# W's transfer ahead of x's, both halves of W's square ahead of x's transposes, and a shorter fourth product of zeros

## The chip, the cores and the metric

The kernel runs on one core of a Trainium2 chip. The metric is the device time of one execution in microseconds (us); a kernel's figure is the median of its runs. TensorE (PE, with its weight loads PEld), VectorE (DVE), ScalarE (ACT) and GpSimd (POOL) compute; SyncE (SP) and ACT issue the transfers here.

## The reference, cut to what matters

x is 128 rows of 256, the context 12544 rows of 256 and W a matrix of 256 by 256. The change lies in the preparation of the first stage, a cross-attention in which queries and keys are projected by the same W and b:

```python
def _L0_xattn_ref(ix, iother, W, b):      # ix = layernorm(x), iother = ctx_1024
    ex = jnp.einsum('bld,ed->ble', ix, W) + b
    eother = jnp.einsum('bld,ed->ble', iother, W) + b
    scores = jnp.einsum('bld,bmd->blm', ex, eother)
    attn = jax.nn.softmax(scores, axis=-1)
    return jnp.einsum('blm,bmd->bld', attn, iother)

x = x + _L0_xattn_ref(_layernorm(x), ctx_1024, W, b)
x = x + _L0_attn_ref(_layernorm(x), proj_w, proj_b, filter_time)   # two gated convolutions
x = x + _L0_ffn_ref(_layernorm(x), norm_g, ..., Wg, bg, Wu, bu, Wd, bd)   # 16 soft experts
```

## The kernel before

The kernel has three stages on 128 partitions. The cross-attention walks the 12544 context rows in 25 groups of up to four tiles of 128 rows, with a running maximum. Instead of projecting every key it projects the queries by WᵀW: `square_W(d)` (L387 to L392) forms half d of WᵀW, with one more column, 256, that gives Wᵀb; for that `W_sb` has 257 columns, of which the last is b, copied there by DVE (L1041, semaphore `bcol_set`). Each half is four records on TensorE in the profile: two products of float32, each recorded twice. ACT copies the first half out of bank 6 with its sign turned (L795), DVE the second half out of bank 7 (L1055); each raises `WW_rdy`. x is normed on DVE (`norm`, L1034 to L1044) with a power on POOL in its middle (`power`, L991), transposed on TensorE (`transpose_xh`, L260 to L266), and copied by DVE into `xhT` (L1053). The query product (L477 to L481) waits for both copies of WW and for `xhT`.

Every engine has its own program, written out by hand; instructions of one engine run in the order written and engines meet at semaphores. The order on TensorE (from L382): four products of zeros into bank 7, each 128 by 256, which only wait for a memset of `zero` (L383 to L385) and whose result nobody reads; then a wait for W's transfer (`ld_W`) and for `bcol_set`, half 0 of the square, a wait for the identity's transfer (`ld_ident`), the two transposes of the normed x (which wait for `xh_rdy`), half 1 of the square, then the transposes of context group 0 (`transpose_ctx`, L474), the query product, the transposes of group 1, and so on. ACT splits group 0's transposes into a high part (`cT_hi`, L807), DVE into a low part (`cT_lo`, L1083); the transposes of group 1 write the same banks 0 and 1 and wait for `cT_lo`.

On SP's queue the order is x (128 KB), W (256 KB), context group 0 (512 KB), then a wait for `ld_W`, groups 1 to 3, the slot embeddings, the filter and the tables (L282 to L297). ACT's queue carries the columns (b among them), the identity and the scale (L783 to L785). POOL's order is memsets, the power of x's norm, then the high and low rows of each group (L1000, L1005). The order on DVE around the change: memsets, x's norm with the copy of b between its parts, the copy of `xhT`, the copy of WW's second half, then `cT_lo` of group 0.

```python
            pe.wait_ge(ld_W, 16)
            pe.wait_ge(bcol_set, 1)
            square_W(0)
            pe.wait_ge(ld_ident, 16)
            transpose_xh(pe, 0)
            square_W(1)
            ...
            transpose_ctx(None, 0, 0)
            pe.wait_ge(WW_rdy, DK)
            pe.wait_ge(xhT_rdy, 1)
```

Of the kernel before, what the change touches and what calls it, by code (L numbers as in the profile page):

```python
# [13 lines left out]
def perceiver_kernel(nc, x, ctx_in, xattn_W, proj_w, proj_b, filter_time, norm_g, norm_b,  # L14
# [3 lines left out]
    ALU = mybir.AluOpType  # L18
# [3 lines left out]
    P = 128  # L22
    D = x.shape[2]
# [28 lines left out]
    with st:  # L52
        def sem(name):
            return st.enter_context(nc.semaphore(name))

        def sb(name, shape, dt=fp32, where=st):
            return where.enter_context(nc.sbuf_tensor(name, shape, dt))

        bank = [st.enter_context(nc.psum_tensor(f"bank{i}", [P, 512], fp32)) for i in range(8)]
# [15 lines left out]
        zero = sb("zero", [P, 1])  # L75
        col = sb("col", [P, 5, DK])
# [44 lines left out]
        W_sb = sb("W_sb", [P, DK, D + 1], fp32, pre)  # L121
        WW = sb("WW", [P, DK, D + 1], fp32, pre)
# [42 lines left out]
        ld_x, ld_W, ld_tab, ld_scale = sem("ld_x"), sem("ld_W"), sem("ld_tab"), sem("ld_scale")  # L165
        ld_se, ld_col, ld_row, ld_filt = sem("ld_se"), sem("ld_col"), sem("ld_row"), sem("ld_filt")
# [12 lines left out]
        WW_ps, WW_rdy = sem("WW_ps"), sem("WW_rdy")  # L179
        bcol_set, bb_rdy, minus_set = sem("bcol_set"), sem("bb_rdy"), sem("minus_set")  # L180
# [79 lines left out]
        def transpose_xh(pe, n):  # L260

            if n == 0:
                pe.wait_ge(xh_rdy, 1)
                for k in range(DK):
                    last = nc.tensor.transpose(bank[XH_BANK[0]][:, k * P:(k + 1) * P], xh[:, k * P:(k + 1) * P], ident)
                last.then_inc(xhT_ps, 1)  # L266
            else:

                for k in range(DK):
                    pe.wait_ge(xh_rdy, k + 2)  # L270
                    nc.tensor.transpose(bank[XH_BANK[1][k]][:, 0:P], xh[:, k * P:(k + 1) * P], ident
                                        ).then_inc(xhT_ps, 1)
# [6 lines left out]

        @block.sync  # L280
        def _(sp):
            sp.dma_start(x_sb[:, :], x[0, :, :]).then_inc(ld_x, 16)  # L282
            sp.dma_start(W_sb[:, :, 0:D], xattn_W.rearrange("(k p) d -> p k d", p=P)).then_inc(ld_W, 16)

            def load_rows(g):
                sp.dma_start(raw[:, g % RING, 0:tiles_of(g), :], ctx_v[:, g * GT:g * GT + tiles_of(g), :]
# [88 lines left out]
        def _(pe):  # L375
# [4 lines left out]


            pe.wait_ge(const_set, 1)  # L382
            for _ in range(4):  # L383
                nc.tensor.matmul(bank[7][:, 0:D], zero[:, 0:1].broadcast_to([P, P]), zero[:, 0:1].broadcast_to([P, D]),  # L384
                                 start=True, stop=True)  # L385

            def square_W(d):  # L387

                for e in range(DK):
                    last = nc.tensor.matmul(bank[6 + d][:, 0:D + 1], W_sb[:, e, d * P:(d + 1) * P], W_sb[:, e, :],  # L390
                                            start=(e == 0), stop=(e == DK - 1))
                last.then_inc(WW_ps, 1)  # L392

            pe.wait_ge(ld_W, 16)
            pe.wait_ge(bcol_set, 1)
            square_W(0)
            pe.wait_ge(ld_ident, 16)
            transpose_xh(pe, 0)
            square_W(1)
            def spectrum(o):  # L400

                pe.wait_ge(ld_filt, 16)
                pe.wait_ge(ld_tab, 16)
                nc.tensor.matmul(bank[4 + o][:, 0:D], dft_s, filt[:, o, :], start=True, stop=True)
                nc.tensor.matmul(bank[4 + o][:, D:2 * D], dft_c, filt[:, o, :], start=True, stop=True
                                 ).then_inc(spec_ps, 1)
# [614 lines left out]
        def _(dve):  # L1021
# [8 lines left out]
            def mean_and_variance(src):  # L1030
                link(nc.vector.bn_stats(stat6[:, :], src))
                link(nc.vector.bn_aggr(mv[:, :], stat6[:, :]))

            def norm(n, src, dst, done):  # L1034

                mean_and_variance(src)
                nc.vector.tensor_scalar(mv[:, 1:2], mv[:, 1:2], EPS, None, ALU.add).then_inc(var_rdy, 1)
                if n == 0:

                    dve.wait_ge(ld_col, 16)  # L1040
                    nc.vector.tensor_copy(W_sb[:, :, D], col[:, 0, :]).then_inc(bcol_set, 1)  # L1041
                dve.wait_ge(rstd_rdy, n + 1)
                nc.vector.tensor_scalar(dst, src, mv[:, 0:1], rstd[:, 0:1], ALU.subtract, ALU.mult
                                        ).then_inc(done, 1)  # L1044
# [2 lines left out]
            nc.vector.memset(minus[:, :], -1.0).then_inc(minus_set, 1)  # L1047
            nc.vector.memset(negm[:, RING - 1:RING], BIG)
            nc.vector.memset(c_hi[:, :, :, D:D + 2].bitcast(fp32), 1.0).then_inc(one_set, 1)
            dve.wait_ge(ld_x, 16)  # L1050
            norm(0, x_sb[:, :], xh[:, :], xh_rdy)
            dve.wait_ge(xhT_ps, 1)
            nc.vector.tensor_copy(xhT[:, :, :].rearrange("p k t -> p (k t)"), bank[XH_BANK[0]][:, 0:D]).then_inc(xhT_rdy, 1)  # L1053
            dve.wait_ge(WW_ps, 2)
            nc.vector.tensor_scalar(WW[:, 1, :], bank[7][:, 0:D + 1], -1.0, None, ALU.mult).then_inc(WW_rdy, 1)  # L1055

# [309 lines left out]
```

## Time and profile before

| | |
|---|---|
| median of 3 runs | 193.16 us (192.81 to 194.14) |
| the profiled execution's own time | 193.59 us |
| its span, first to last instruction | 191.5 us |
| PE / PEld busy | 187.1 us (98%) / 146.8 us (77%) |
| DVE / ACT / POOL busy | 125.7 / 108.8 / 82.3 us |
| DMA | 47.01 MB, mean 245 GB/s |

Some 2.1 us of an execution lie outside the span. A busy PE counts overlapping records of pipelined matmuls, whose ends are modelled; the starts of successive records are the better measure of pace, and this document steps from start to start.

### The profile page before, as it was taken

The page shows a single profiled execution, that of the slowest core. Times are in us where ns is not written, and L with a number is a line of the kernel's source. Part 1 is how long each engine was busy: PE and PEld are TensorE (multiplying, and loading weights), DVE is VectorE, ACT ScalarE, POOL GpSimd, SP SyncE. Part 2 cuts the span into 40 slices and gives each one's busy share as a digit, 9 for nine tenths or more (in the row PEclk, how much of TensorE's full clock was granted, in tenths as well). Part 3 has the DMA queues.
Part 4 walks back from the last instruction along what each step waited for, and adds up shares of the span by engine and source line. Part 5 has one row for each costly group of instructions (what it writes and reads, how often), then busy time and mean ns, then how long its engine had stood idle before and what let it go on. Part 6 is the DMA issues. An engine that isn't in the chain of part 4 may idle for free.

```text
span 191.5 us, 3972 instructions
## 1 busy us (share of the span) xinstructions
PE 187.1 (98%) x1270; PEld 146.8 (77%) x1270; DVE 125.7 (66%) x272; ACT 108.8 (57%) x226; POOL 82.3 (43%) x61
## 2 busy tenths in 40 slices
PE   8999999999999999999999999999999999999995
PEld 5888999999999999999999989974544545454463
DVE  3376997797778779777778788753673513524542
ACT  3558778777777776776775542967358521112210
POOL 2678879778778768877868013100000000000000
DMA  6999958857874774985594299999999999992200
GB/s 183 317 364 334 336 162 265 264 179 219 237 241 158 272 262 147 324 225 161 154 235 106 74 381 379 354 371 369 381 364 383 285 348 296 282 216 79 83 0 27
DMA packets 25051, 47.01 MB, mean 245 GB/s; under 512 B 1616, under 2 KB 12112, under 8 KB 25040
## 3 DMA queue, kind: packets, MB, share of 16 engines
q1 hardware_dynamic: 23808, 43.52, 70.2%
q10 hardware_dynamic: 1232, 3.35, 7.1%
q8 instruction: 6, 0.10, 0.2%
q14 instruction: 5, 0.04, 0.1%
HBM read 46.73 MB, written 0.13 MB: 245 GB/s over the span
## 4 chain that ended last, share of the span: by engine, by line
PE 95%; ACT 2%; DVE 1%; issue 0%; POOL 0%; ACTq 0%; POOLq 0%
PE bank L670 15%; PE bank L415 11%; PE bank L684 6%; PE bank L456 6%; PE bank L460 6%; PE bank L458 6%; PE bank L428 6%; PE bank L432 6%; PE bank L430 6%; PE bank L441 6%; PE bank L732 2%; PE bank L722 2%; PE bank L384 2%; PE bank L557 2%; PE bank L576 2%; ACT seT L888 1%
## 5 line engine op out<-in xcount | busy, mean ns | idle before, releaser
L1005 POOL TENSOR_TENSOR c_lo<-raw,c_hi 128x1024 fp32r<-128x1024 f32 (+1 forms) x25 | 53.9, 2156 | 20.9 <-ACT c_hi L801 20.9
L1083 DVE TENSOR_TENSOR cT_lo<-bank,cT_hi 128x512 fp32r<-128x512 f32 (+1 forms) x50 | 31.7, 674 | 9.7 <-ACT cT_hi L828 8.6
L828 ACT ACTIVATE cT_hi<-bank 128x512 fp32r<-128x512 f32 (+1 forms) x48 | 25.6, 584 | 9.8 <-PE bank L415 9.7
L456 PE MATMUL bank<-c_hi,pT_hi 128*128 128x258 f32 x98 | 30.0, 306 | 0.0
L460 PE MATMUL bank<-c_hi,pT_lo 128*128 128x258 f32 x98 | 27.7, 283 | 0.0
L458 PE MATMUL bank<-c_lo,pT_hi 128*128 128x256 f32 x98 | 27.6, 281 | 0.0
L1000 POOL TENSOR_TENSOR c_hi<-raw,zero 128x512 fp32r<-128x512 f32 (+1 forms) x25 | 25.6, 1025 | 1.5 <-DMA raw<-in_ctx_dram 1.5
L415 PE MATMUL bank<-tab,raw 128*128 128x128 f32 x196 | 25.6, 273 | 0.2 <-DVE cT_lo L1083 0.2
L835 ACT ACTIVATE pT_hi<-bank 128x512 fp32r<-128x512 f32 (+1 forms) x25 | 14.7, 590 | 14.5 <-PE bank L441 14.5
L415 PEld LDWEIGHTS bank<-tab,raw 128*128 128x128 f32 x196 | 22.1, 141 | 0.8 <-issue 0.3
L428 PE MATMUL bank<-cT_hi,q_hi 128*128 128x512 f32 (+1 forms) x50 | 21.5, 430 | 0.0
L1101 DVE TENSOR_TENSOR pT_lo<-bank,pT_hi 128x512 fp32r<-128x512 f32 (+1 forms) x25 | 17.0, 679 | 5.2 <-ACT pT_hi L835 5.0
L1095 DVE TENSOR_SCALAR_CACHE_REDUCE nsc<-bank,s,negm 128x512 f32<-128x512 f32 (+1 forms) x25 | 19.8, 793 | 0.8 <-PE bank L432 0.7
L843 ACT ACTIVATE prob<-nsc,negm 128x512 f32<-128x512 f32 (+1 forms) x25 | 17.7, 710 | 3.3 <-DVE nsc L1095 2.9
L432 PE MATMUL bank<-cT_hi,q_lo 128*128 128x512 f32 (+1 forms) x50 | 19.5, 390 | 0.0
L430 PE MATMUL bank<-cT_lo,q_hi 128*128 128x512 f32 (+1 forms) x50 | 19.3, 386 | 0.0
L458 PEld LDWEIGHTS bank<-c_lo,pT_hi 128*128 128x128 f32 x98 | 18.7, 191 | 0.0
L460 PEld LDWEIGHTS bank<-c_hi,pT_lo 128*128 128x128 f32 x98 | 18.5, 189 | 0.0
L456 PEld LDWEIGHTS bank<-c_hi,pT_hi 128*128 128x128 f32 x98 | 18.5, 189 | 0.0
L801 ACT ACTIVATE c_hi<-raw 128x512 fp32r<-128x512 f32 (+1 forms) x25 | 15.6, 625 | 0.0
L670 PE MATMUL bank<-early_gu,slots_or_se 128*64 128x512 f32 x64 | 15.2, 600 | 0.0
L1111 DVE SCALAR_TENSOR_TENSOR O<-O,alpha,bank 128x258 f32<-128x258 f32 x25 | 12.1, 482 | 4.3 <-PE bank L460 2.9
(178 smaller groups left out, 292.7 us busy)
## 6 DMA issues: line engine op xcount, KB each, us to landing
raw<-in_ctx_dram SPq DMA_DIRECT2D x24, 512.0 KB, 3.9
bias<-biases_dram ACTq DMA_DIRECT2D x10, 320.0 KB, 7.5
late_gu<-in_L_ffn_Wg_dram SPq DMA_DIRECT2D x3, 1024.0 KB, 10.5
late_gu<-in_L_ffn_Wu_dram SPq DMA_DIRECT2D x3, 1024.0 KB, 11.2
late_d<-in_L_ffn_Wd_dram SPq DMA_DIRECT2D x3, 1024.0 KB, 13.7
early_gu<-in_L_ffn_Wg_dram SPq DMA_DIRECT2D x4, 512.0 KB, 4.7
early_gu<-in_L_ffn_Wu_dram SPq DMA_DIRECT2D x4, 512.0 KB, 4.6
early_d<-in_L_ffn_Wd_dram SPq DMA_DIRECT2D x4, 512.0 KB, 5.0
```

Source lines behind the costliest of these rows:

```text
L415: last = nc.tensor.transpose(bank[h][:, t * P:(t + 1) * P], raw[:, slot, t, h * P:(h + 1) * P], ident)
L428: nc.tensor.matmul(bank[2 + r][:, 0:n], q_hi[:, h, :], cT_hi[:, r, h, 0:n], start=(h == 0), stop=False)
L430: nc.tensor.matmul(bank[2 + r][:, 0:n], q_hi[:, h, :], cT_lo[:, r, h, 0:n], start=False, stop=False)
L432: last = nc.tensor.matmul(bank[2 + r][:, 0:n], q_lo[:, h, :], cT_hi[:, r, h, 0:n], start=False, stop=(h == DK - 1))
L456: nc.tensor.matmul(bank[6 + r][:, 0:D + 2], ph, c_hi[:, slot, t, :], start=(t == 0), stop=False)
L458: nc.tensor.matmul(bank[6 + r][:, 0:D], ph, c_lo[:, slot, t, :], start=False, stop=False)
L460: last = nc.tensor.matmul(bank[6 + r][:, 0:D + 2], pl, c_hi[:, slot, t, :], start=False, stop=(t == nt - 1))
L670: last = nc.tensor.matmul(bank[b][a * SL:(a + 1) * SL, :], slotsT[:, k, p * P + a * SL:p * P + (a + 1) * SL], w_gu(s, which, a, a + 1)[:, ...
L828: nc.scalar.activation(cT_hi[:, g % 2, h, 0:n], bank[h][:, 0:n], ACT.Copy).then_inc(cThi_rdy, 1)
L1000: nc.gpsimd.tensor_tensor(c_hi[:, slot, 0:nt // 2, 0:D], raw[:, slot, 0:nt // 2, :], zero[:, 0:1].unsqueeze(2).broadcast_to([P, nt // 2, D ...
L1005: nc.gpsimd.tensor_tensor(c_lo[:, slot, 0:nt, :], raw[:, slot, 0:nt, :], c_hi[:, slot, 0:nt, 0:D].bitcast(fp32), ALU.subtract).then_inc(cl ...
L1083: nc.vector.tensor_tensor(cT_lo[:, g % 2, h, 0:n], bank[h][:, 0:n], cT_hi[:, g % 2, h, 0:n].bitcast(fp32), ALU.subtract).then_inc(cTlo_rdy, 1)
```

## The change

W's transfer is issued before x's on SP. On TensorE the fourth product of zeros streams 64 columns instead of 256, and half 1 of the square comes before the transposes of x. On DVE the copy of b into `W_sb` comes before the wait for x, and the copy of WW's second half before the copy of `xhT`. Transfers, products and copies are otherwise the same ones.

```diff
         def _(sp):
+            sp.dma_start(W_sb[:, :, 0:D], xattn_W.rearrange("(k p) d -> p k d", p=P)).then_inc(ld_W, 16)
             sp.dma_start(x_sb[:, :], x[0, :, :]).then_inc(ld_x, 16)
-            sp.dma_start(W_sb[:, :, 0:D], xattn_W.rearrange("(k p) d -> p k d", p=P)).then_inc(ld_W, 16)
...
             pe.wait_ge(const_set, 1)
-            for _ in range(4):
-                nc.tensor.matmul(bank[7][:, 0:D], zero[:, 0:1].broadcast_to([P, P]), zero[:, 0:1].broadcast_to([P, D]),
+            for w in (D, D, D, P // 2):
+                nc.tensor.matmul(bank[7][:, 0:w], zero[:, 0:1].broadcast_to([P, P]), zero[:, 0:1].broadcast_to([P, w]),
                                  start=True, stop=True)
...
             square_W(0)
+            square_W(1)
             pe.wait_ge(ld_ident, 16)
             transpose_xh(pe, 0)
-            square_W(1)
...
                 nc.vector.tensor_scalar(mv[:, 1:2], mv[:, 1:2], EPS, None, ALU.add).then_inc(var_rdy, 1)
-                if n == 0:
-
-                    dve.wait_ge(ld_col, 16)
-                    nc.vector.tensor_copy(W_sb[:, :, D], col[:, 0, :]).then_inc(bcol_set, 1)
...
+            dve.wait_ge(ld_col, 16)
+            nc.vector.tensor_copy(W_sb[:, :, D], col[:, 0, :]).then_inc(bcol_set, 1)
             dve.wait_ge(ld_x, 16)
             norm(0, x_sb[:, :], xh[:, :], xh_rdy)
+            dve.wait_ge(WW_ps, 2)
+            nc.vector.tensor_scalar(WW[:, 1, :], bank[7][:, 0:D + 1], -1.0, None, ALU.mult).then_inc(WW_rdy, 1)
             dve.wait_ge(xhT_ps, 1)
             nc.vector.tensor_copy(xhT[:, :, :].rearrange("p k t -> p (k t)"), bank[XH_BANK[0]][:, 0:D]).then_inc(xhT_rdy, 1)
-            dve.wait_ge(WW_ps, 2)
-            nc.vector.tensor_scalar(WW[:, 1, :], bank[7][:, 0:D + 1], -1.0, None, ALU.mult).then_inc(WW_rdy, 1)
```

## Rows read from the trace of the kernel before

**Rows 1.** The page: the chain that ended last, by engine.

```profile
PE 95%; ACT 2%; DVE 1%; issue 0%; POOL 0%; ACTq 0%; POOLq 0%
```

**Rows 2.** Waits of PE's matmuls over the whole span: total us, times, longest.

```profile
PE bank L384 <- POOL neg_half L985: 0.9, 1, 0.9
PE bank L518 <- ACT xhT L877: 0.3, 1, 0.3
...
PE bank L415 <- DVE cT_lo L1083: 0.2, 1, 0.2
```

**Rows 3.** Timeline of PE, 0 to 20 us: start, us, line, tiles, count [idle before].

```profile
0.90 3.78 PE L384 MATMUL bank<-zero 128*128 128x256 f32 x8 [0.90 <-POOL neg_half L985]
...
6.46 1.03 PE L390 MATMUL bank<-W_sb 128*128 128x257 f32 x4
7.34 1.04 PE L415 MATMUL bank<-tab,raw 128*128 128x128 f32 x8
8.21 1.06 PE L479 MATMUL bank<-xhT,WW 128*128 128x128 f32 x8
9.44 1.16 PE L415 MATMUL bank<-tab,raw 128*128 128x128 f32 x8 [0.17 <-DVE cT_lo L1083]
10.44 0.50 PE L487 MATMUL bank<-WW,xhT 128*128 128x1 f32 x4
...
11.25 0.48 PE L428 MATMUL bank<-cT_hi,q_hi 128*128 128x512 f32 x1
```

**Rows 4.** Timelines of PE over short windows: the starts of single records.

```profile
3.62 1.06 PE L384 MATMUL bank<-zero 128*128 128x256 f32 x2
...
4.04 0.64 PE L384 MATMUL bank<-zero 128*128 128x256 f32 x1
4.48 0.50 PEld L390 LDWEIGHTS bank<-W_sb 128*128 128x128 f32 x2 [0.53 <-DMA W_sb<-in_L_xattn_W_dram]
...
5.07 1.07 PE L390 MATMUL bank<-W_sb 128*128 128x257 f32 x2
...
5.93 0.48 PE L390 MATMUL bank<-W_sb 128*128 128x257 f32 x1
6.25 0.27 PE L265 MATMUL bank<-tab,xh 128*128 128x128 f32 x1
```

**Rows 5.** Timeline of DVE, 0 to 20 us.

```profile
2.86 0.43 DVE L1031 BATCH_NORM_STATS2 stat<-x_sb 128x6 f32<-128x256 f32 x1 [1.52 <-DMA x_sb<-in_x_dram]
...
4.43 0.41 DVE L1043 TENSOR_SCALAR xh<-x_sb,mv,rstd 128x256 f32<-128x256 f32 x1 [0.67 <-POOL rstd L991]
...
7.54 0.42 DVE L1055 TENSOR_SCALAR WW<-bank 128x257 f32<-128x257 f32 x1 [0.45 <-PE bank L390]
8.60 1.29 DVE L1083 TENSOR_TENSOR cT_lo<-bank,cT_hi 128x512 fp32r<-128x512 f32 x2 [0.64 <-ACT cT_hi L807]
```

**Rows 6.** Timelines of POOL and ACT in the same stretch.

```profile
5.91 1.04 POOL L1000 TENSOR_TENSOR c_hi<-raw,zero 128x512 fp32r<-128x512 f32 x1 [1.51 <-DMA raw<-in_ctx_dram]
...
7.97 1.08 ACT L807 ACTIVATE cT_hi<-bank 128x512 fp32r<-128x512 f32 x2 [0.62 <-PE bank L415]
```

**Rows 7.** Timeline of SP's queue: when transfers are issued.

```profile
0.75 0.39 SPq L282 DMA_DIRECT2D x_sb<-in_x_dram  x1
1.20 0.42 SPq L283 DMA_DIRECT2D W_sb<-in_L_xattn_W_dram  x1
```

**Rows 8.** DMA issues, 0 to 14 us: KB each, us from issue to landing.

```profile
W_sb<-in_L_xattn_W_dram SPq DMA_DIRECT2D x1, 256.0 KB, 3.2
...
x_sb<-in_x_dram SPq DMA_DIRECT2D x1, 128.0 KB, 2.1
tab<-tables_dram ACTq DMA_DIRECT2D x1, 64.0 KB, 3.3
col<-columns_dram ACTq DMA_DIRECT2D x1, 5.0 KB, 2.3
```

**Rows 9.** Busy time by stretch; the last three columns: granted clock, DMA share, GB/s.

```profile
2.00:3.00 1.00, 1.00 (x4) 0.82 (x3) 0.14 (x1) 0.81 (x1) 0.00 (x0) 1.00 0.92 144
```

## The prediction

> **What bounds the kernel now.** I read the chain of work that ended last first: TensorE carries 95% of the span [rows 1]. Then the waits of its matmuls: the listed ones are five, none over 0.3 us after the start, and none of them is for a transfer [rows 2]. So what is gained or lost ahead of the steady loop over the context groups should reach the end, and only TensorE's own time counts, or a stall of it. That sends the reader to its timeline over the first 20 us [rows 3]: it works without a gap from 0.90 us to the transposes of group 1 at 9.44, where it waits 0.17 us for the low part of group 0.
>
> The second thing to see is its pace. The granted clock is shown as 1.00 throughout [rows 9], but equal records tell otherwise. Products of 256 or 257 columns start 0.42 to 0.43 us apart before 6 us (3.62 to 4.04; 5.07 to 5.93 for two [rows 4]) and the four records of the square's second half take 6.46 to about 7.34, 0.22 us each [rows 3]. That is TensorE at 1.2 GHz and then at 2.4 GHz. The last slow record starts at 5.93 and the transpose behind it at 6.25: 0.32 us, a mixture of both paces. With a share s at 0.43 and the rest at 0.217, s/0.43 + (0.32 - s)/0.217 = 1 gives s = 0.21, so the clock rose at about 6.14 us, after 5.24 us of work. A microsecond saved in front of that moment is filled with other slow work until it comes: only half of it is left behind it, if the moment itself stands still.
>
> The third thing is W. The weight load of the square's first record waits 0.53 us for the transfer and starts at 4.48; the next record starts at 5.07, 0.59 us after it and not 0.43 [rows 4]. A load that waits can't be done ahead, which costs 0.16 us. W is issued at 1.20 and lands 3.2 us later, at 4.40; x is issued at 0.75 and lands 2.1 us later, at 2.85 [rows 7, 8].
>
> **The fourth product of zeros.** Its two records start at 3.62 and 4.04 [rows 4], together 0.85 us. With 64 columns the stream would be a quarter, 0.107 us each. But every record also loads 128 columns of weights, which doesn't shrink. The nearest rows for that floor are the products with one column: eight records (L487 and L489, four each) start between 10.44 and 11.25, 0.10 us each at 2.4 GHz [rows 3], so 0.20 at 1.2 GHz. I take the floor: 2 x 0.20 = 0.41, a saving of 0.44 us at the slow pace; the other bound is 0.85 - 0.21 = 0.64. The zeros then end at 3.62 + 0.41 = 4.03 us. The Trainium skill ("TensorE: Matmul & The Clock Gate", LDWEIGHTS) prices a load by its columns alone, 128/1.2 = 107 ns, which would be no floor here and give the 0.64; the rows of this kernel show 0.10 us already at the full clock for a float32 record with almost no stream, so I stay with them.
>
> **W first.** Issued at 0.75 in place of 1.20, W lands at 0.75 + 3.2 = 3.95 us at the latest, if being first in the queue saves nothing. If it does: x, half its size, landed after 2.1 us, and the second 128 KB take another 0.9 us at the 144 GB/s that the stretch from 2 to 3 us moved [rows 9]: 0.75 + 2.1 + 0.9 = 3.75 us. The lower bound is x's own landing, 2.85. I take 3.75. The column b, which used to be copied in the middle of x's norm, needs its own transfer: ACT issues it first, it takes 2.3 us [rows 8], and DVE is free until x comes, so the copy of two elements per partition is done near 3.3 us. Both are then there before the load of the square's first record can begin (3.83, when the last zero record starts), and the 0.16 us goes as well. The square's second record starts at 4.03 + 0.43 = 4.46 in place of 5.07: 0.61 us earlier, all at the slow pace. With W at 3.95 it starts at 3.95 + 0.59 = 4.54, 0.53 us earlier. With no gain of W at all it starts at 5.07 as before: the zeros are only filler, and the whole saving hangs on W.
>
> **Both halves before the transposes.** This moves work and removes none. By 6.14 us, (6.14 - 4.03)/0.433 = 4.87 of the square's eight records are done; the other 3.13 take 0.68 us at 0.217, to 6.82; the two transposes take 0.21 us (6.25 to 6.46 [rows 3, 4]), to 7.03. The transposes of group 0 then start at 7.03 and not at 7.34: a gain of 0.30 us, half of 0.61.
>
> **What is later, and what hides it.** x is now behind W in the queue. It lands at 3.3 us at the earliest (1.20 + 2.1) and at 4.40 at the latest, since both transfers together were through by then. From landing to the normed x it takes 2.86 to 4.84, 1.98 us, with the power on POOL in it [rows 5]; so the normed x is there between 5.3 and 6.4 us. The cover is the square, until 6.82: 0.4 us at least. Without it TensorE would stand until 6.4, and POOL's power, queued ahead of group 0's high rows at 5.91 [rows 6], would hold those by under 0.1 us, which ACT's later half hides (POOL's low part needs ACT's rows as well). The identity is unmoved and lands at 4.5, 3.3 us after its issue on ACT [rows 8].
>
> DVE has two copies of 0.42 us in a row: WW's second half from 7.03 (0.2 us behind the last record, as now: 7.34 to 7.54 [rows 3, 5]) to 7.45, then `xhT` to 7.87. The query product waits for both. TensorE reaches it at 7.03 + 0.87 = 7.90 (7.34 to 8.21 [rows 3]), and a waiting weight load costs up to 0.2 us: 8.1 us, ending by 9.0. Behind it stand the transposes of group 1, which must wait anyway for `cT_lo` of group 0: that chain runs from the transposes of group 0 over ACT at 7.97 and DVE at 8.60 to 9.44 [rows 3, 5, 6], and all of it moves up by the 0.30, to 9.14. So the small stall lies inside a wait that exists, and I cost it at nothing. ACT copies the first half of WW earlier than before. Groups 1 to 3 are issued behind the wait for `ld_W`, some 0.6 us earlier; TensorE waits for none of them now, and group 0 is issued third as before. From 9.44 on TensorE has no wait of its own until the next stage [rows 2], so the 0.30 stays to the end.
>
> **The sum.** 193.59 - 0.30 = 193.29 us for the profiled execution, which lies 0.43 above the median of the runs; against that median 193.16 - 0.30 = 192.86, say 192.9 us. Bounds of the mechanism: 0.26 (half of 0.53) to 0.80 (0.64 + 0.16, if the clock doesn't rise until all of it is banked).
>
> **Rivals.** *Nothing gained*: W's landing is set by what else the engines carry (the identity, the columns and group 0 share them), or TensorE waits for x or for DVE instead. For it: W took 3.2 us though its bytes are few. Against it: x alone landed 1.55 us before W. The start of the square stays at 4.48, and the time at 193.2.
>
> *The clock rises later.* The zeros are there to keep TensorE at work; with a shorter fourth one the activity in front of 6.14 is thinner (two records that mostly load weights), and where W comes late it even stands still from 4.03 on. If that starts the count anew, the clock rises 5.24 us after 4.03, at 9.3 us and not at 6.14; the 3.1 us run at half pace, a loss of 1.57, less the 0.30: +1.3, or 194.4 us. Being over 1% slower would need 4.5 us more at 1.2 GHz. Against it: the load of W's first record at 4.48 left a thin place too, and the clock rose all the same. The Trainium skill ("TensorE: Matmul & The Clock Gate", Why this matters for your kernels) advises keeping TensorE at work without a pause until its clock is released, which speaks against shortening filler; no row here shows a rise missed for one short product.
>
> *The clock rises earlier.* The gap at W's load and the transposes are out of the first 6 us, which is then denser in products. If the clock rose as early as 4.03, (6.14 - 4.03)/2 = 1.05 us would come on top of 0.30: 191.8 us, still not 1% faster. But x would then be needed at 5.8 us and could be late, taking back up to 0.6. No row speaks for a rise that early.
>
> **How the numbers follow.** Forecast, 0.26 to 0.80 faster: 0.62. Nothing gained: 0.18. Later rise, 194.4: 0.12. Earlier rise, 191.8: 0.06. Something unnamed: 0.02. The runs of before spread from 0.35 below to 0.98 above their median. The range takes in the forecast's far bound with the spread below, 193.16 - 0.80 - 0.35 = 192.0, and the no-gain case with the spread above, 193.16 + 0.98 = 194.1. It leaves out the last three cases, 0.20. About 1% (1.9 us) is what a measurement of this kernel can tell from no change. No named case crosses it on either side; the tails of the clock's rivals give 0.03 faster and 0.04 slower, and 0.93 stays within 1%.
>
> **What the profile would show.** Right: SP's first transfer is W, landed by 3.95; the last zero record 0.2 us after the one before it; the square's first record near 4.0 with no weight load waiting for W; eight records of the square in a row, then the transposes of x near 6.8 with no wait for x; group 0's transposes near 7.0, group 1's near 9.1, and every later start 0.3 us earlier. Wrong: a wait of TensorE for W until 4.4, or for x; group 1's transposes gated by the query product; or records of the square, of group 0 or of the queries at the slow pace beyond 6.2 us.

## The result, and the profile after

The changed kernel takes 194.31 us (median of 18 runs, 193.65 to 194.66), the kernel before 193.22 us (median of 18 runs, 192.72 to 194.14). The ratio is 1.0045, with a 95% interval of 1.0033 to 1.0058: slower by some 0.9 us (the means of the runs differ by 0.92, the medians by 1.09), where 0.3 us faster was forecast. The profiled execution took 194.36 us with a span of 192.3 us, 0.77 and 0.8 us above those of before.

The timeline of PE of the changed kernel, 0 to 20 us:

```profile
0.90 3.25 PE L384 MATMUL bank<-zero 128*128 128x256 f32 x8 [0.90 <-POOL neg_half L985]
3.94 2.70 PE L390 MATMUL bank<-W_sb 128*128 128x257 f32 x8
6.48 0.41 PE L265 MATMUL bank<-tab,xh 128*128 128x128 f32 x2
8.00 1.09 PE L415 MATMUL bank<-tab,raw 128*128 128x128 f32 x8 [1.12 <-DMA raw<-in_ctx_dram]
8.93 1.06 PE L479 MATMUL bank<-xhT,WW 128*128 128x128 f32 x8
10.17 1.16 PE L415 MATMUL bank<-tab,raw 128*128 128x128 f32 x8 [0.17 <-DVE cT_lo L1082]
```

Down to 6.48 us this is what was forecast, and better: no pause before W, the square in one piece from 3.94, the transposes of x at 6.48 with no wait. Then TensorE, which would have been at group 0 by 6.7, stands 1.12 us for the transfer of group 0. Its transposes start at 8.00 in place of 7.34, those of group 1 at 10.17 in place of 9.44 [rows 3], and 0.73 us is, within 0.1, what the span has grown.

The rest of the kernel follows that start closely. In 13 of the 20 profiles of this study the span ends 184.2 to 184.3 us after group 0's transposes begin, whatever the order of the transfers (191.5 - 7.34 before, 192.3 - 8.00 here); in the other seven group 1 was late too, or TensorE's clock was still low. So the start of these transposes is the figure to compare. By it the kernel before, at its median of 193.22 us, has them near 6.9 us (an estimate: 193.22 less the 2.1 us outside the span, less 184.2); its profiled execution, with 7.34, was one of its slower ones. The changed kernel has them at 8.0 by its median too.

The chain that ended last, for the first 11 us (start, us, what), shows the same from the other end:

```profile
0.75 0.45 SPq L282
...
1.26 0.47 SPq L283
...
1.78 6.18 DMA raw<-in_ctx_dram
...
8.00 0.67 PE bank L415 x4
```

The chain of before was on TensorE from 0.90 us. Now it runs through SP's first two issues and the third transfer, group 0: 6.18 us from issue to landing. In the kernel before, POOL, which was waiting for it, could start on group 0 at 5.91 [rows 6]. SP's queue and the landings of W and x in the changed kernel (the second fence is the list of issues: KB each, us to landing):

```profile
0.75 0.45 SPq L282 DMA_DIRECT2D W_sb<-in_L_xattn_W_dram  x1
1.26 0.47 SPq L283 DMA_DIRECT2D x_sb<-in_x_dram  x1
3.84 1.28 SPq L286 DMA_DIRECT2D raw<-in_ctx_dram  x3
5.16 0.65 SPq L294 DMA_DIRECT2D slots_or_se<-n_L_ffn_slot_embeds_dram  x1
```

```profile
W_sb<-in_L_xattn_W_dram SPq DMA_DIRECT2D x1, 256.0 KB, 3.1
x_sb<-in_x_dram SPq DMA_DIRECT2D x1, 128.0 KB, 3.1
```

W lands at 3.85 and frees SP's wait behind group 0: groups 1 to 3 are issued from 3.84 us on. In the kernel before W landed at 4.40 [rows 7, 8], and the same stretch of SP's timeline reads:

```profile
4.45 1.28 SPq L286 DMA_DIRECT2D raw<-in_ctx_dram  x3
```

So two things have changed around group 0: W's longer transfer goes ahead of x's, and three transfers of 512 KB are issued 0.6 us sooner behind it. The busy table by stretch (last columns: granted clock, DMA share, GB/s) shows that the engines moved less while group 0 was due; first the changed kernel, then the one before:

```profile
4.00:5.00 1.00, 1.00 (x4) 0.81 (x4) 0.61 (x2) 0.06 (x1) 0.00 (x0) 1.00 0.51 176
5.00:6.00 1.00, 1.00 (x5) 0.86 (x4) 0.24 (x2) 0.19 (x1) 0.56 (x1) 1.00 1.25 291
```

```profile
4.00:5.00 1.00, 1.00 (x3) 0.50 (x2) 0.41 (x1) 0.06 (x1) 0.40 (x1) 1.00 1.00 389
5.00:6.00 1.00, 1.00 (x4) 0.74 (x3) 0.00 (x0) 0.00 (x0) 0.09 (x1) 1.00 0.86 140
```

Between 4 and 5 us, when most of group 0 must have come in before (W landed at 4.40 and group 0 by 5.9), the changed kernel moves 176 GB/s in place of 389.

### The profile page after: what moved, and what is told of

It reads as the page before. It is cut to its first block, busy times and chain, and to the rows that moved or that the text cites. A ratio compares the mean times of both kernels' runs of the same rounds, so it can differ in the third digit from the quotient of the medians.

```text
span 192.3 us, 3972 instructions
## 1 busy us (share of the span) xinstructions
PE 186.7 (97%) x1270; PEld 146.6 (76%) x1270; DVE 125.7 (65%) x272; ACT 108.9 (57%) x226; POOL 82.3 (43%) x61
## 4 chain that ended last, share of the span: by engine, by line
PE 92%; DMA 3%; ACT 2%; DVE 1%; SPq 0%; issue 0%; ACTq 0%
PE bank L670 15%; PE bank L415 11%; PE bank L684 6%; PE bank L456 6%; PE bank L460 6%; PE bank L458 6%; PE bank L428 6%; PE bank L432 6%; PE bank L430 6%; PE bank L441 6%; DMA raw<-in_ctx_dram 3%; PE bank L732 2%; PE bank L722 2%; PE bank L557 2%; PE bank L576 2%; ACT seT L888 1%
```

## The experiments

The theory to test: the loss is group 0's landing, and that is late through the order of transfers, not through TensorE's new order or the shorter product. Within it two causes compete: (A) the issue of groups 1 to 3 at 3.8 in place of 4.45 us, and (B) W's transfer ahead of x's by itself. The landings of group 0 below are the starts of the first instructions that waited for it; where none waited (d1, d4, f1) they are the issue plus the time that the list of issues gives. "Changed" and "before" are the two kernels of this document; ratios are to the kernel before, from the same chip.

**Is it the order of transfers?** Two kernels take the change apart.

```diff
 # c1_swap: the kernel before, with
+            sp.dma_start(W_sb...)      # ahead of x
             sp.dma_start(x_sb...)
 # and on DVE, ahead of the wait for x
+            dve.wait_ge(ld_col, 16)
+            nc.vector.tensor_copy(W_sb[:, :, D], col[:, 0, :]).then_inc(bcol_set, 1)
```

> The kernel before with only W's transfer ahead of x's, and the copy of b into W_sb ahead of the wait for x (without it the square would wait for x). TensorE's order and the four full products of zeros are those of before. Theory (W first, or what is issued behind it, makes group 0 late): group 0 lands near 8.0 us as in the changed kernel and not at 5.9, TensorE waits for it up to 1.1 us, the time is 0.6 to 1.1 us above before. Rival (TensorE's new order or the shorter product is at fault): group 0 lands by 6.3, and the time is within 0.2 us of before.

194.04 us, ratio 1.0036 (1.0017 to 1.0054). Group 0 lands at 7.70. But TensorE's long wait is another one here: the transposes of x still stand between the halves of the square, and x is late.

```profile
4.47 1.38 PE L390 MATMUL bank<-W_sb 128*128 128x257 f32 x4
6.45 0.41 PE L265 MATMUL bank<-tab,xh 128*128 128x128 f32 x2 [0.60 <-DVE xh L1039]
7.68 1.09 PE L415 MATMUL bank<-tab,raw 128*128 128x128 f32 x8
```

TensorE waits 0.60 us for the normed x; group 0, landed at 7.70, costs it only some 0.1 on top. But the two waits cover each other: without the first, TensorE would have been at group 0 by 7.0 and waited there instead, so it is still group 0's landing that sets the 7.68. The swap costs time without the rest of the change. The expected size came out; the expected wait of up to 1.1 us shows as two.

```diff
 # c2_no_swap: the changed kernel, with
             sp.dma_start(x_sb...)
+            sp.dma_start(W_sb...)      # behind x again
```

> The changed kernel with x's transfer ahead of W's again; the shorter product and both halves of the square ahead of the transposes stay. Theory (the order of transfers is the cause): group 0 lands at about 5.9, TensorE does not wait for it, and the time is that of before within 0.3 us. Rival (the order on TensorE): the time stays about 0.9 us above before.

193.56 us, ratio 1.001 (0.9982 to 1.0038). Group 0 lands at 6.13, no wait for it; TensorE stands 0.32 us for W.

```profile
4.47 2.76 PE L390 MATMUL bank<-W_sb 128*128 128x257 f32 x8 [0.32 <-DMA W_sb<-in_L_xattn_W_dram]
...
7.29 1.04 PE L415 MATMUL bank<-tab,raw 128*128 128x128 f32 x8
```

The changed kernel differs from this one by the swap alone, and it is what loses. The loss is gone with the swap, and so is the gain: TensorE's new order and the shorter product alone bring nothing that this can measure.

**Which of the two causes?**

```diff
 # c3_hold_next: the changed kernel
             load_rows(0)
             sp.wait_ge(ld_W, 16)
+            sp.wait_ge(ld_raw[0], 16)
             load_rows(1)
```

> The changed kernel, but SP issues groups 1 to 3 only when group 0 has landed. Theory A (groups 1 to 3, issued 0.6 us earlier than before behind the wait for W, share the DMA engines with group 0): group 0 lands at 6.0 to 6.5, its transposes start by 7.1, and the time is 0.8 to 1.1 us below the changed kernel unless group 1 is then late. Theory B (W's longer transfer ahead holds group 0 itself): group 0 still lands at 7.5 to 8 and the time is that of the changed kernel or worse.

196.62 us (six runs, 194.56 to 198.06), ratio 1.0115 (1.0068 to 1.0162). Group 0 lands at 7.13: between the two answers. Holding the others back gives 0.9 of the 2.1 us and leaves 1.2 over the kernel before (d3 below, with the same hold, brings what W ahead of x costs down to 0.5). Group 1, issued at 7.19, is then late, and behind that pause TensorE's clock falls:

```profile
11.14 1.09 PE L416 MATMUL bank<-tab,raw 128*128 128x128 f32 x8 [2.00 <-DMA raw<-in_ctx_dram]
...
13.67 0.63 PE L431 MATMUL bank<-cT_lo,q_hi 128*128 128x512 f32 x1
14.10 0.63 PE L433 MATMUL bank<-cT_hi,q_lo 128*128 128x512 f32 x1
```

Products of 512 columns start 0.43 us apart behind the 2.00 us wait; the same two start 0.24 us apart in the changed kernel (12.29 and 12.53). That is 1.2 GHz again (granted clock 0.50 from 13 to 15 us). The length of the pause alone does not decide it: in d1 and d4 below, waits of 2.21 and 2.48 us have no such fall behind them.

```diff
 # c4_no_hold: the kernel before
             load_rows(0)
-            sp.wait_ge(ld_W, 16)
             load_rows(1)
```

> The kernel before without SP's wait for W ahead of group 1, so that groups 1 to 3 are issued from about 2.2 us on; transfer order and all else as before. Theory A (early issue of groups 1 to 3 delays group 0): group 0 lands at 7.5 us or later, TensorE waits for it, the time is 0.8 us or more above before. Theory B (W ahead of x is what delays group 0): group 0 lands near 5.9 and the time is within 0.2 us of before.

193.97 us, ratio 1.0039 (1.0017 to 1.006). With x first and all as before, but groups 1 to 3 issued from 2.17 us on, group 0 is late too:

```profile
7.53 1.09 PE L414 MATMUL bank<-tab,raw 128*128 128x128 f32 x8 [0.68 <-DMA raw<-in_ctx_dram]
```

So early issue alone can delay group 0 from 5.91 to 7.5 us (A), though these issues are 1.7 us earlier than the changed kernel's, and the time was expected 0.2 us higher than it came.

```diff
 # d2_hold_x: the changed kernel
             sp.wait_ge(ld_W, 16)
+            sp.wait_ge(ld_x, 16)
             load_rows(1)
```

> The changed kernel with SP waiting for x as well as for W ahead of group 1: groups 1 to 3 are issued at about 4.35 us, where the kernel before issues them at 4.45 us. If the early issue alone costs the time, group 0 lands near 6 and the time is within 0.3 us of before or below it. If W ahead of x costs by itself, group 0 lands between 7.1 (what holding groups 1 to 3 to the end gave) and 7.7, and the time is 0.4 to 0.7 us above before.

193.8 us, ratio 1.0034 (1.0005 to 1.0062). Groups 1 to 3 are issued at 4.33, and group 0 lands at 6.80, between the two answers and 1.2 us earlier than in the changed kernel, for issues 0.5 us later; its transposes start at 7.02 with no wait for it or for x.

```profile
5.85 0.41 DVE L1040 TENSOR_SCALAR xh<-x_sb,mv,rstd 128x256 f32<-128x256 f32 x1 [0.74 <-POOL rstd L992]
7.02 1.04 PE L416 MATMUL bank<-tab,raw 128*128 128x128 f32 x8
6.84 1.04 POOL L1001 TENSOR_TENSOR c_hi<-raw,zero 128x512 fp32r<-128x512 f32 x1 [1.03 <-DMA raw<-in_ctx_dram]
10.96 1.09 PE L416 MATMUL bank<-tab,raw 128*128 128x128 f32 x8 [1.92 <-DMA raw<-in_ctx_dram]
```

The 7.02 is what the prediction had forecast (7.03), with the clock rising near 6.0 as it had assumed. But this execution (196.64 us, the highest of the twelve) then waits 1.92 us for group 1. Nine of the twelve lie between 193.24 and 194.20. The lateness can move from group 0 to group 1; what holds the nine back no profile shows.

```diff
 # d3_before_hold: the kernel before
             sp.wait_ge(ld_W, 16)
+            sp.wait_ge(ld_raw[0], 16)
             load_rows(1)
```

> The kernel before with groups 1 to 3 held until group 0 has landed: the same hold as in the changed kernel, now with x ahead of W. If W ahead of x costs by itself, group 0 lands here at 5.5 to 6.0 against 7.1 there. If not, it lands at about 7 here too. Group 1 is then late in either case, and the whole time 1.5 to 3 us above before.

196.02 us (one run). Group 0 lands at 6.60, between the answers again and 0.7 us later than in the kernel before, though nothing is issued behind it before 6.65. The hold itself need not be the cause: between 4.00 and 4.25 us, before it acts, the engines moved 98 GB/s here and 360 in the kernel before. Against 7.13 with W first it is still 0.5 us earlier.

```diff
 # e1_hold_23: the changed kernel; e2_before_hold_23: before; e3_no_swap_hold_23: changed, x first
             load_rows(1)
+            sp.wait_ge(ld_raw[0], 16)
             load_rows(2)
```

> The changed kernel; SP issues group 1 behind the wait for W as there, but groups 2 and 3 and all behind them only when group 0 has landed. If it is the mass of groups 2, 3 and the slot embeddings that holds group 0, group 0 lands near 7.0 us, group 1 near 8, TensorE waits for neither, and the time is 0.2 to 0.5 us below before. If group 1 alone holds group 0, it still lands at 7.5 to 8 and the time stays 0.5 us or more above before.

193.97 us, ratio 1.0041 (1.0023 to 1.0059). Group 0 lands at 7.70 and TensorE waits 0.69 us for it: with group 1 alone behind it, issued at 3.70, it is about as late as with all three (7.7 to 8.0). The mass of groups 2 and 3 falls as a cause.

> The kernel before with the same hold of groups 2 and 3. TensorE waits for neither group 0 nor group 1 in the kernel before, so nothing is to be gained: within 0.3 us of before. Were it 0.3 us or more faster, the hold and not the change's order would be the gain of its sister kernel.

193.06 us, ratio 0.9998 (0.9981 to 1.0015): nothing gained, as expected. Group 0 lands at 6.44.

> The changed kernel with x ahead of W and the same hold of groups 2 and 3. W lands at 4.4 us, so the square starts as in before; group 0's transposes near 7.3. Expected within 0.3 us of before and 0.2 to 0.4 us slower than the kernel with W ahead and the same hold, if W's earlier landing is worth what the prediction said.

193.36 us, ratio 1.0017 (0.9991 to 1.0043), group 0 at 6.59. It was to be slower than its sister with W ahead and is not, since that one still waits for group 0.

> The changed kernel as it is, once more, to see how far the landing of group 0 moves between executions. If its lateness is systematic, group 0 lands between 7.5 and 8.3 us again and TensorE waits 0.6 to 1.4 us for it; if it was one execution's chance, it lands below 7.1 and there is no wait.

194.16 us (one run), span 192.1. Group 0 lands at 7.87 and TensorE waits 1.20 us: systematic. Its clock rose a microsecond earlier than in the first profile (5.5 and 4.4 us), and its span is only 0.2 us shorter.

```profile
6.28 0.41 PE L265 MATMUL bank<-tab,xh 128*128 128x128 f32 x2 [0.15 <-DVE xh L1039]
7.89 1.09 PE L415 MATMUL bank<-tab,raw 128*128 128x128 f32 x8 [1.20 <-DMA raw<-in_ctx_dram]
```

The landings of group 0 together:

| order | next issue at | group 0 lands |
|---|---|---|
| x first (before, c2, f2, f3; e2, e3, d3 with a hold) | 4.34 to 4.75, d3 6.65 | 5.9, 6.1, 6.0, 5.9; 6.4, 6.6, 6.6 |
| x first (c4) | 2.17 | 7.5 |
| W first (d2, c3) | 4.33, 7.19 | 6.8, 7.1 |
| W first (changed, e4, c1, e1) | 3.70 to 3.92 | 8.0, 7.9, 7.7, 7.7 |

Kernels with the same program on SP agree within 0.3 us (5.9 to 6.1 for four of them, 7.7 to 8.0 for three), so these differences are not one execution's chance; but with x first and a hold the group lands 0.3 to 0.7 us later than without one, which no run explains. Issue before 4 us costs about 0.9 us with W first; W first costs about 0.7 us at a late issue. TensorE wants the group at 6.7 to 7.3. Either cause alone about reaches that; both exceed it.

**Can W be early and group 0 in time?** Three other orders.

```diff
 # d1_x_on_act: the changed kernel
 # SP
-            sp.dma_start(x_sb[:, :], x[0, :, :]).then_inc(ld_x, 16)
 # ACT
             act.dma_start(col[:, :, :], columns).then_inc(ld_col, 16)
+            act.dma_start(x_sb[:, :], x[0, :, :]).then_inc(ld_x, 16)
 # f1_x_act_first: the same, the two lines of ACT the other way round
 # d4_x_third: the changed kernel, on SP
-            sp.dma_start(x_sb[:, :], x[0, :, :]).then_inc(ld_x, 16)
...
             load_rows(0)
+            sp.dma_start(x_sb[:, :], x[0, :, :]).then_inc(ld_x, 16)
```

> The changed kernel with x's transfer issued on ACT's queue (columns, x, identity, scale); SP issues W and then group 0. If what stands ahead of group 0 in SP's own queue makes it late, group 0 lands up to 1.2 us earlier than in the changed kernel (near 6.8), and with TensorE's new order the time is at or up to 0.3 us below before. If only the total ahead on the 16 engines and the early issue of groups 1 to 3 count, group 0 lands at 7.5 to 8 and the time stays 0.5 to 0.9 us above before.

194.13 us, ratio 1.0046 (1.003 to 1.0062). Group 0, issued at 1.26, takes 4.1 us and lands near 5.4, better than ever, but x, issued on ACT's queue, takes 4.3 us, and TensorE waits for it:

```profile
x_sb<-in_x_dram ACTq DMA_DIRECT2D x1, 128.0 KB, 4.3
```

```profile
8.42 0.41 PE L265 MATMUL bank<-tab,xh 128*128 128x128 f32 x2 [2.21 <-DVE xh L1039]
```

> The changed kernel with the order W, group 0, x on SP. If the many small rows ahead of group 0 (W's 256 KB and x's 128 KB in pieces of 1 KB) hold it, group 0's first rows start by 3.3 us instead of 3.9 and it lands by 7.0. If not, it lands at 7.5 or later. In both cases x lands after group 0 has taken its share, near 5 to 6 us, and TensorE waits for the normed x.

195.23 us (one run), span 193.1: the same from SP's queue. Group 0 lands near 5.5, x at 5.87, and TensorE waits 2.48 us for the normed x.

> The changed kernel with x issued first on ACT's queue (ahead of the columns), at the same moment as W on SP, so that group 0 is the second and not the third transfer on SP and is issued at 1.26 us. Theory (group 0 is late because of what is ahead of it in its queue and of the early issue of groups 1 to 3): group 0 lands at 7.1 us or earlier, x by 4.5, and with no wait the time is 0.0 to 0.4 us below before. If x and W now hold each other up (W at 4.3 or later, or x at 5.3 or later as when ACT issued it second), TensorE waits for W or x and the time is 0.3 us or more above before.

196.07 us, ratio 1.0157 (1.0123 to 1.019). The highest ratio of all (by the median c3's 196.62 is higher). Group 0 lands near 5.9 and x by 4.4, as the theory had it, and W at 4.6, as its rival had it; what costs the time is a transfer that nobody had priced: the 5 KB of the columns, which hold b, are now second on ACT's queue and take 4.8 us, where they took 2.3 [rows 8]. The square waits for b:

```profile
6.41 2.74 PE L389 MATMUL bank<-W_sb 128*128 128x257 f32 x8 [2.27 <-DVE W_sb L1048]
```

The Trainium skill ("DMA: Bandwidth & Descriptors", Issuing engines are not separate DMA queues) says that transfers issued by SP and ACT share the same 16 engines; these rows agree, since x issued on ACT was held by group 0 of SP as much as x behind it in the same queue (4.3 and 4.1 us).

**The clock.** The profiles of kernels with a pause before W showed it rising late. The single records give the moment:

```diff
 # f2_short_only: the kernel before, with
+            for w in (D, D, D, P // 2):        # the shorter fourth product
 # f3_order_only: the changed kernel, x first, four full products of zeros
```

> The kernel before with only the fourth product of zeros shortened. TensorE then stands about 0.4 us for W before the square. If a pause there can delay the rise of the clock, some of the executions are 1.5 us or more above the median (195 us and more; the kernel before has none above 194.14) and the rest within 0.2 us of before. If it can't, all executions stay within the spread of before.

192.94 us, ratio 0.9998 (0.9974 to 1.0023). Ten of twelve lie between 192.85 and 193.82; two at 195.08 and 195.23. The first of these is the profiled one:

```profile
4.70 2.08 PE L390 MATMUL bank<-W_sb 128*128 128x257 f32 x4 [0.55 <-DMA W_sb<-in_L_xattn_W_dram]
6.57 0.64 PE L265 MATMUL bank<-tab,xh 128*128 128x128 f32 x2
6.99 1.92 PE L390 MATMUL bank<-W_sb 128*128 128x257 f32 x4
8.71 1.17 PE L415 MATMUL bank<-tab,raw 128*128 128x128 f32 x8
```

The second half of the square, 0.88 us before [rows 3], takes 1.72 (6.99 to 8.71): the clock rose at about 9.0 us and not near 6. A pause of 0.55 us in front of W precedes it. Of twelve executions two are that slow, though the cut product should leave a pause in all of them.

> The kernel before with only the order changed: both halves of the square ahead of the transposes, DVE's copies to match; x's transfer first and four full products of zeros. Work is only moved, so the median is within 0.2 us of before, and with no pause before W no execution lies above 194.6 us if pauses cause the late ones.

193.27 us, ratio 1.002 (0.9996 to 1.0044). Two of twelve lie at 194.64 and 194.71, just over the line that was drawn. Its profiled execution (192.75 us, span 190.7) has the clock high by 4.77 us and group 0's transposes at 6.51:

```profile
4.47 1.98 PE L390 MATMUL bank<-W_sb 128*128 128x257 f32 x8
6.29 0.38 PE L265 MATMUL bank<-tab,xh 128*128 128x128 f32 x2
6.51 1.04 PE L415 MATMUL bank<-tab,raw 128*128 128x128 f32 x8
```

Counted over the kernels: with x first and the shorter product (c2, e3, f2, g3), TensorE pauses before W, and 14 of 48 executions lie above 194.6 us. With x first and four full products (f3, e2, g1) it is 2 of 36, and none of the 18 of the kernel before, nor of its 128 further runs beside the experiments (highest 194.11). That makes the pause a likely cause, not a certain one: the two of f3 had no profile, and c4, with four full products as well, has two of twelve at 195.06 and 195.19, which its wait for group 0 does not account for.

**Is the wait for group 0 the whole loss?** The last three kernels make it impossible for group 0 to be late: they load one of its four tiles, 128 KB, and put zeros into the other three.

```diff
 # g1_before_small0, g2_after_small0, g3_no_swap_small0 (changed, x first)
-            load_rows(0)
+            sp.dma_start(raw[:, 0, 0:1, :], ctx_v[:, 0:1, :]).then_inc(ld_raw[0], 16)
 # DVE:
+            nc.vector.memset(raw[:, 0, 1:GT, :], 0.0).then_inc(raw0_set, 1)
 # TensorE, ACT and POOL wait for raw0_set ahead of group 0
```

> The kernel before with a quarter of group 0's transfer (one tile of four, 128 KB; the other three tiles are set to zero by DVE, so their rows take no real part in the result). Group 0 lands well before TensorE wants it. TensorE did not wait for group 0 before, so the time is within 0.3 us of before. It is the base for the next kernel.

192.83 us (192.53 to 193.51), ratio 0.9983 (0.9965 to 1.0): a little faster than expected.

> The changed kernel with the same quarter of group 0 (three of its four tiles are zeros, not read from the context). Theory (the whole loss is the wait for group 0, and the prediction's gain was real behind it): no wait for group 0, its transposes near 6.5 to 7.0 us, and the time 0.2 to 0.8 us below the kernel before with the same quarter. Rival (W first or TensorE's order costs in another way too): the time is at or above that kernel's.

193.35 us (193.14 to 193.6), ratio 1.0 (0.9985 to 1.0015), 0.52 us above g1 by the medians and 0.39 by the means. The forecast's theory fails here: group 0 is in time and the change still loses, with group 0's transposes at 7.30 where g1 has them at 6.91. The profile names the next wait, and its cause:

```profile
3.96 2.38 PE L391 MATMUL bank<-W_sb 128*128 128x257 f32 x8
7.05 0.41 PE L266 MATMUL bank<-tab,xh 128*128 128x128 f32 x2 [0.70 <-DVE xh L1043]
7.30 1.04 PE L416 MATMUL bank<-tab,raw 128*128 128x128 f32 x8
```

```profile
5.78 1.12 DVE L1043 TENSOR_SCALAR xh<-x_sb,mv,rstd 128x256 f32<-128x256 f32 x1 [0.74 <-POOL rstd L994]
```

```profile
5.19 0.56 POOL L994 TENSOR_TENSOR rstd<-mv,neg_half 128x1 f32<-128x1 f32 x1 [4.17 <-DVE mv L1041]
5.71 1.04 POOL L1003 TENSOR_TENSOR c_hi<-raw,zero 128x512 fp32r<-128x512 f32 x1
```

The last step of x's norm takes 1.12 us where it took 0.41 [rows 5]. POOL, just done with the power, finds group 0 landed and starts on its high rows at 5.71; the step on DVE, issued at 5.78, lasts beyond POOL's end. In d1, d4 and f1, where x is late and group 0 is not, it takes 1.12 us each time as well; in every kernel where POOL is idle at that moment it takes 0.41. In g3 the order is the other way round, DVE at 4.75 and POOL's rows at 4.95: there the step takes 0.41 and POOL's rows 1.11 in place of 1.04. The Trainium skill ("SBUF — State Buffer", Who interferes with whom) says that a float32 operation of DVE of such a kind can hold, or wait for, a port pair that it shares with GpSimd, whole instruction against whole instruction; the four traces agree, in that the step outlasts POOL's each time (6.90 against 6.75 in g2).

This wait belongs to g2 more than to the change. A quarter of group 0 is there at 4.9 us, before POOL has finished the power, so its rows start at once; in the changed kernel and in d2, where group 0 lands at 8.0 and 6.8, the step takes 0.41. Without the 0.70 us the transposes of group 0 would start near 6.6 in g2 (an estimate, 7.30 - 0.70), 0.3 ahead of g1, though TensorE's clock also rose some 0.5 us earlier in this profile. A gain of the forecast's size may well be there, up to the next wait; no run shows it clear of that.

> The changed kernel with x ahead of W and the same quarter of group 0. TensorE stands 0.4 to 0.6 us for W behind the shortened zeros, nothing is gained by them: median within 0.3 us of the kernel before with the quarter and 0.2 to 0.6 us above the one with W ahead; single executions near 195 us where the clock rises late.

194.16 us (192.61 to 195.62), ratio 1.0023 (0.999 to 1.0057). Two bunches: six executions at 192.6 to 193.6, six at 194.7 to 195.6, the latter with the late clock (its profiled one, 194.98, has all eight records of the square at the slow pace, 4.54 to 8.13). By the median it is 0.8 above g2, more than expected; its better half is no slower than g2, and four of its runs (192.61 to 192.77) are faster than any of g2's.

No kernel of the study is clearly faster than the one before.

## Why the prediction was wrong, point by point

- **What bounds the kernel.** Right: a shift ahead of the loop reaches the end. Group 0's transposes start at 6.51, 7.34, 8.00 and 8.71 in f3, before, changed and f2; the spans are 190.7, 191.5, 192.3 and 193.0. But "only TensorE's own time counts, or a stall of it" was followed up for W and x alone.
- **The fourth product.** Mis-sized, though it cost nothing. Its two records start at 3.62 and 3.72 us, 0.10 apart, which is the pace of the stream alone (0.107) and not the 0.20 of the weight-load floor that I took; the other bound, a saving of 0.64, was the better one. By the price per column that the Trainium skill ("TensorE: Matmul & The Clock Gate", LDWEIGHTS) gives, a load of 128 columns takes an estimated 107 ns, no floor here, and the 0.10 us between the starts agree with it; the recorded loads are longer (0.34 us each at this pace), but overlap the products. The square's first record starts at 3.94 (4.03 forecast), now behind the landing of W at 3.85.
- **W first.** Right: landed at 3.85, between the 3.75 taken and the bound of 3.95; the square's second record starts at 4.47 (4.46 forecast).
- **Both halves before the transposes.** Right in direction: the transposes of x start at 6.48 (6.82 forecast). Part of that is luck. The sum had the clock rise at 6.14 whatever came before it; it rose at about 5.5 us in this execution and near 4.4 in e4, and kernels with W's order of before have it as early as 4.3 (c4, e2).
- **x behind W.** Landed at 4.34 (at most 4.40 forecast), normed by 6.33 as POOL was idle. The cover was named as the square, 0.4 us at least. It is smaller when the clock rises early: e4, the same kernel, waits 0.15 us for an x that landed at 4.14. And where group 0 is there before POOL is done with the power, it is too small as well: the norm ends at 6.9 (g2), since the collision of its last step with POOL's high rows was not in the sum. The text saw POOL's power delay those rows, and not that the rows can delay the norm.
- **The step that failed: "Groups 1 to 3 are issued ... some 0.6 us earlier; TensorE waits for none of them now, and group 0 is issued third as before."** The earlier issue was costed at nothing, and so was the new order of the two transfers ahead of group 0: "issued third as before" was taken for landing as before. It was right about when (3.84 for 4.45) and about the groups that it moved, and forgot the one already under way. With x first again (c2) group 0 lands at 6.13 and TensorE doesn't wait for it; with W first but the next issue 0.5 us later (d2) it lands at 6.80 and TensorE doesn't wait for it either. TensorE had 7.34 - 5.91 = 1.4 us of slack on group 0, 1.1 after the forecast gain; the landing moved by 2.1. One term was missing from the sum: 1.12 us of waiting, from 6.88 us, which was 0.46 us ahead of the old 7.34; that leaves +0.66 at group 0's transposes, and ACT, which now copies group 0's rows (0.63 us from 7.98) directly in front of `cT_hi`, makes it 0.73.
- **Rivals.** *Nothing gained* was closest: it named the sharing with group 0 and a wait of TensorE for x, but let them cost the gain and no more; it had W as the victim, and it was group 0. *The clock rises later* is real, though not in the changed kernel, whose TensorE has no pause before W and whose two profiles have it at about 5.5 and 4.4 us; it belongs to the shorter product without W first (f2, e3, g3), and costs more than the 1.3 us worked out: 195.1 to 195.2 against 192.9 in f2 is 2.2. *The clock rises earlier* happens too, and gains nothing in the changed kernel, since the wait for group 0 takes it up: which would explain that 14 of its 18 runs lie between 194.10 and 194.47.
- **The range** ended at 194.1 because its upper end was the case of no gain with the spread above. A rival of a transfer that arrives late for TensorE, with its own price, would have carried it past the measured time: 193.16 + 0.73 (the delay measured) + 0.98 (the spread above) is 194.9.

Open is why W ahead of x delays group 0 by 0.5 us when nothing is issued behind it (c3 against d3) and by 0.7 to 0.9 with the next issue near 4.4 (d2 against the kernels with x first). With group 0 second instead of third it lands at 5.4 to 5.9, so the place in the queue counts; why the same bytes ahead of it should cost more in the other order, no run here tells.

## What to carry to other kernels

Moving a transfer forward moves everything that waits behind its semaphore: for each such issue ask what is under way at that moment and how much slack it has, not only who needs the issued one. At the start of this kernel the transfers are a chain of deadlines (W by 3.9, x before 4.2, group 0 by 6.7 and group 1 by 9 us), and an order that relieves one breaks the next; an engine that is 95% of the chain still has a limit to its cover. Filler that keeps TensorE at work up to the landing of its first operand is better not cut to end before it, unless the operand comes earlier for certain.

## What the runs showed of the hardware that was not expected

- A 512 KB transfer that had landed 4.2 us after its issue took 6.2 when another of its size was issued behind it 0.6 us sooner and the two small ones ahead of it changed places (5.91 and 7.98 us). The engines moved 176 GB/s from 4 to 5 us, where they had moved 389.
- A transfer of 5 KB took 4.8 us from its issue as the second of ACT's queue (f1), where it takes 2.3 to 3.0 as the first.
- A float32 step of DVE went from 0.41 to 1.12 us when POOL had just begun on its rows, in four kernels of four, and stayed at 0.41 where the step began first (g3).
- The moment at which TensorE goes from 1.2 to 2.4 GHz moves by itself: from about 4.3 us (c4, e2) to 6.1 us (before) with work from 0.90 us on. Behind a pause of 0.40 to 0.63 us before W three profiles have it at 9.0 to 9.7 us; another, c2, behind 0.32 us, at 6.1.
